# Group 0 taken in one piece before group 1's row work: an order change at the head of a routed expert layer

## The reference

```
x  = x + layernorm(x) @ W          # W: 256 x 256, set from the edge list (src, dst, weight)
z  = layernorm(x)
xn = layernorm(z) * gamma + beta
w  = softmax of the 2 largest of (xn @ Wr + br), 0 for the other 6 experts
x  = x + sum over e of w[e] * (gelu(xn @ W1[e] + b1[e]) @ W2[e] + b2[e])
```

## Time and profile before

| | |
|---|---|
| median of 3 runs | 1067.41 us (1066.4 to 1067.57) |
| the profiled execution | 1067.55 us, its span 1065.8 us |
| busy, share of the span | PE 85%, PEld 79%, DVE 71%, ACT 59%, POOL 59% |
| stretch of the 196 sends on POOL | 139.6 to 390.7 us |
| third stage on PE | from 395.9 us to the end |
| mean granted TensorE clock | 0.919 of full speed |

### The profile page before, as it was taken

One profiled execution on the slowest core, in us unless ns is written; L12 is line 12 of the kernel. 1 busy time (PEld: TensorE's weight loads), 2 busy tenths in 40 slices (PEclk: granted clock), 3 DMA queues, 4 the chain that ended last, 5 costly groups with the idle time before them and its releaser, 6 DMA issues. The chain is left out here.

```text
span 1065.8 us, 25585 instructions
## 1 busy us (share of the span) xinstructions
PE 902.6 (85%) x6756; PEld 842.6 (79%) x6757; DVE 753.5 (71%) x2311; ACT 633.5 (59%) x1324; POOL 630.5 (59%) x490
## 2 busy tenths in 40 slices
PE   1494698898986109999999999999999999999991
PEld 1123577777765109999999999999999999999991
DVE  4995798999984606777777777777777777777761
ACT  2244567666654006667667667667677677677661
POOL 3645057777777752465655655655756565656653
PEclk9797798989986559999999999999999999999996
DMA  4144457757654443465554554554654554555542
GB/s 123 56 127 150 135 161 228 225 195 243 210 168 158 148 162 72 73 99 87 82 95 73 93 94 80 82 96 73 93 92 79 83 95 79 92 85 81 93 67 30
DMA packets 95923, 121.47 MB, mean 114 GB/s; under 512 B 15198, under 2 KB 73734, under 8 KB 95752
## 3 DMA queue, kind: packets, MB, share of 16 engines
q0 software_dynamic: 39904, 53.56, 29.1%
q1 hardware_dynamic: 55976, 67.43, 21.9%
HBM read 51.94 MB, written 69.00 MB: 113 GB/s over the span
## 5 line engine op out<-in xcount | busy, mean ns | idle before, releaser
L574 POOL DMA_INDIRECT out_dram<-ysb,yid x210 | 382.6, 1822 | 283.6 <-ACT ysb L1342 132.9
L744 PE MATMUL psum<-xh,w1s 128*128 128x256 f32 x1680 | 310.9, 285 | 0.0
L744 PEld LDWEIGHTS psum<-xh,w1s 128*128 128x128 f32 x1680 | 257.1, 189 | 0.0
L558 POOL DMA_INDIRECT slots<-arena_z,pos x196 | 191.8, 978 | 89.8 <-issue 58.8
L757 PE MATMUL psum<-w2h,hl 128*128 x840 | 237.5, 283 | 0.0
L757 PE MATMUL psum<-w2l,hh 128*128 x840 | 237.3, 283 | 0.0
L757 PE MATMUL psum<-w2h,hh 128*128 x840 | 237.2, 282 | 0.0
L744 PE MATMUL psum<-xl,w1s 128*128 128x256 f32 x840 | 235.3, 280 | 0.0
L1159 DVE TENSOR_TENSOR hl<-hact,hh 128x512 fp32r<-128x512 f32 x210 | 145.6, 693 | 88.0 <-ACT hh L1206 87.8
L1206 ACT ACTIVATE xh<-psum 128x512 fp32r<-128x512 f32 x105 | 62.7, 597 | 221.3 <-PE psum L731 221.3
L1325 ACT ACTIVATE hact<-psum,b1T 128x256 f32<-128x256 f32 x420 | 174.5, 466 | 14.2 <-PE psum L744 2.8
(11 more groups left out here) (186 smaller groups left out, 1123.8 us busy)
## 6 DMA issues: line engine op xcount, KB each, us to landing
zin<-slots SPq DMA_DIRECT2D x105, 260.0 KB
arena_x<-in_x_dram SPq DMA_DIRECT2D x14, 512.0 KB, 5.4
out_dram<-arena_s SPq DMA_DIRECT2D x14, 512.0 KB
arena_z<-in_L_ffn_W_dram SPq DMA_DIRECT2D x24, 256.0 KB, 2.8
arena_x<-in_x_dram SPq DMA_DIRECT2D x13, 384.0 KB
out_dram<-arena_s SPq DMA_DIRECT2D x13, 384.0 KB
out_dram<-ysb,yid POOLq DMA_INDIRECT x210, 4.3
slots<-arena_z,pos POOLq DMA_INDIRECT x196
```

Source lines behind the costliest of these rows:

```text
L558: pool.indirect_dma_start(slots[:, :], bass.IndirectOffsetOnAxis(ap=pos[b][0:n, k, s:s + 1], axis=0), zg[b][0:n, s, :], None).then_inc(sen ...
L574: pool.indirect_dma_start(out[:, :], bass.IndirectOffsetOnAxis(ap=yid[u % MB][:, n:n + 1], axis=0), ysb[u % YB][:, n, :], None, compute_op ...
L744: last = nc.tensor.matmul(bank[2 + 2 * b + q][:, m * PAIR:(m + 1) * PAIR], w1s[b][:, w, k, hb * P:(hb + 1) * P], xs[b][:, k * PAIR:(k + 1) ...
```

## The change

On each of three engines the order of groups 0, 1 and 2 is rewritten; nothing is computed otherwise. PE does group 0's whole z side right behind its x side, then the first half of group 1's x side with `ranks(0)` in it, then the rest. DVE does group 0 with nothing filled in, then `x_scales` of group 1, the route and the place of group 0, each as one run, and then group 1 with `x_scales` of group 2 filled in and no route. Group 2 holds the route of group 1 and no place; group 3 holds the place of group 1, as it did. ACT follows PE. SP's and POOL's programs are not touched.

```diff
@@ PE
-            group(1, 1, older=False)
-            for g in range(2, GROUPS):
+            for q in range(NP):
+                turn_z(0, q, 0)
+                if q > 0:
+                    logits(0, q - 1)
+            logits(0, NP - 1)
+            turn_x(1, 0)
+            turn_x(1, 1)
+            edge_product(1, 0)
+            ranks(0)
+            turn_x(1, 2)
+            turn_x(1, 3)
+            for q in range(1, NP):
+                edge_product(1, q)
+            group(2, 0, older=False)
+            for g in range(3, GROUPS):
@@ DVE
-                scales = iter(()) if last else x_scales(g + 1, 1 - b, loads)
-                router = iter(()) if first else route(g - 1, (g - 1) % RZ)
-                places = iter(()) if g < 2 else place(g - 2, (g - 2) % RZ)
+                scales = iter(()) if first or last else x_scales(g + 1, 1 - b, loads)
+                router = iter(()) if g < 2 else route(g - 1, (g - 1) % RZ)
+                places = iter(()) if g < 3 else place(g - 2, (g - 2) % RZ)
...
             group(0, 0, first=True)
+            for steps in (x_scales(1, 1), route(0, 0), place(0, 0)):
+                for _ in steps:
+                    pass
             group(1, 1)
@@ ACT
-            group(1, 1, older=False)
-            for g in range(2, GROUPS):
+            act.wait_ge(z_scale_ready, 1)
+            for s in range(4):
+                z_norm(0, s, 0)
+            z_copy(0, 0)
+            z_norm(0, 4, 0)
+            z_norm(0, 5, 0)
+            z_copy(0, 1)
+            z_norm(0, 6, 0)
+            z_copy(0, 2)
+            z_copy(0, 3)
+            act.wait_ge(x_scale_ready, 2)
+            for s in range(3):
+                x_norm(1, s, 1)
+            x_copy(1, 0)
+            x_norm(1, 3, 1)
+            x_norm(1, 4, 1)
+            x_copy(1, 1)
+            exp_gap(0)
+            x_norm(1, 5, 1)
+            x_norm(1, 6, 1)
+            x_copy(1, 2)
+            x_copy(1, 3)
+            group(2, 0, older=False)
+            for g in range(3, GROUPS):
```

## The result

The changed kernel takes 1077.8 us (median, 1076.97 to 1078.44) against 1067.49 us before (1065.48 to 1068.36) in the same comparison: a ratio of 1.0098 [1.0085, 1.0111], slower by 1%. The forecast was 1076.5 us, between 1070.5 and 1080. The profiled execution of the changed kernel took 1077.85 us with a span of 1076.1.

The account below looks back on a forecast made before the run. POOL's unbroken sends were taken to bound the group stage. Stretches up to group 1's first send summed to 166.6 against 157.5, +9.1 us: 1067.55 + 9.1 = 1076.65, set at 1076.5 us against the median, range 1070.5 to 1080.

Parts of the forecast that it names:

- The bound and the one-for-one end: POOL's unbroken sends limit the group stage; the kernel's end moves one for one with the last send.
- Steps 1 to 5: Group 0's statistics, z side, route, ranks and place run alone: released at 129.0 instead of 138.67, 9.7 us earlier.
- step 1: Group 0's statistics and root on DVE end at 110.0, bounds 109.3 and 110.8; stall beside POOL 0.7 us at most.
- Step 6: On DVE, group 1's adds stand behind group 0's place: x_scale_ready at 137.8, 8.8 us after group 0's release.
- Steps 7 and 8: Group 1 released at 165.7, sent at 166.6; POOL idle from 147.8, never starving again; end moves +9.1 us.
- step 7: From group 1's x_scale_ready to its release, with group 2's work between: 27.9 us, bounds 24.5 and 29.
- Rival B: PE reaches 2.4 GHz sooner: half or more, 1065.4 to 1069.5, chance 0.08; less than half, 1069.6 to 1073, 0.15.
- The lower bounds: Fast ends at 2.4 GHz: z side 5.6 us, product and ranks 4.5, x_scale_ready to group 1's release 24.5.
- step 2: Group 0's z side alone on PE and ACT: 10.2 us at 1.2 GHz, 5.6 us at 2.4 GHz.
- B's full case: All of PE's work in the lower bounds at 2.4 GHz: -2.1 us, 1065.4; chance 0.08 together with about half of it.

Follow-up runs that it names:

- hold_first_sends: The changed kernel with POOL's sends of group 0 held until group 1's z scale is ready: 1077.44 us, ratio 1.0083 to the kernel before.
- route_place_spread: The changed kernel with DVE filling in group 0's route and place as before, PE and ACT unchanged: 1076.58 us, ratio 1.007 to the kernel before.
- the last kernel: The changed kernel with extra products on PE behind group 0, ahead of group 2 and in the gaps: 1069.78 us, ratio 1.0007 to the kernel before.

## Why the prediction was right

**The bound and the one-for-one end.** It said that the end moves with group 1's first send and not with group 0's. hold_first_sends shows it: group 0's first send moved by 11 us, and the time stayed. route_place_spread moved it by 20, to where POOL just ran without a break again, and the time did not rise either. Group 1's send moved by 10.36 us and the profiled time by 10.3.

**Steps 1 to 5.** S at 110.96, against 110.0; the first stage's own shift is 1.2 us, so without it S would lie 0.2 us ahead of the forecast. Five steps of the root took 1.12 to 1.20 us instead of 0.17 beside POOL's subtractions, the stall that step 1 allowed for. The z side alone took 121.15 - 110.96 = 10.19 us (forecast 10.2). `chosen_ready` came at 125.0 (L1001 ran from 124.7, 0.29 long), forecast 124.1 from a route at 120.3, the same 3.8 us. The ranks were waited for 2.56 us, forecast 3, and the place took 1.65 (forecast 1.8). Group 0 was released at 129.54, forecast 129.0. Taking the price of a stretch from the one place in the old trace where the same work ran alone and at the same clock, group 13's, was what made these come out.

**Step 6.** From group 0's release to `x_scale_ready`: 138.17 - 129.54 = 8.63 us, forecast 8.8. The size was right, its cause only in part. I said that the place, with its wait for the ranks, holds group 1's adds. route_place_spread shows the adds waiting for PE as long, less about 1.4 us: PE's second product would not have been there sooner. The hold is on PE and ACT, which begin group 1's x side at 120.96 and 119.07 instead of 111.97 and 110.83.

**Steps 7 and 8.** 138.17 to 167.04 is 28.87 us, forecast 27.9, bounds 24.5 and 29: near the slow bound, with the clock at 0.57 in the middle of it. DVE waited there for ACT's z norms (4.24 us) and not for the loads that moved. POOL was idle for 19.77 us, forecast 166.6 - 147.8 = 18.8, and no second hole followed. Group 1's send at 167.86 against 166.6: S lay 1.0 us later, step 7 took 1.0 more, the steps between 0.7 less.

**Rival B, tested by force.** The lower bounds (5.6, 4.5 and 24.5 us) would have put group 1's send at 155.4. With PE at 2.4 GHz from 100 to 165 us it came at 158.58 from an S of 109.92. Two of the three bounds held: from the logits' end to the ranks 122.59 - 118.05 = 4.5 us, and from `x_scale_ready` (132.87) to the release (157.76) 24.9. The second of these held by a looser working than the first: it halved the whole 6.5 us, the waits for ACT with them. The z side's did not hold: 118.05 - 109.92 = 8.1 us and not 5.6. Halving PE's busy time leaves ACT's chain of norms and copies, whose last copy ends at 116.33, 6.4 us after S, with the last logits still to come. A part of the 8.1 us is the extra products themselves, which stand in the z side's gaps; how much was not measured. So the term that was mis-sized is the lower bound of step 2: in this form B's full case was worth 1069.8 us and not 1065.4.

**How much is order and how much is clock.** With PE kept busy in both kernels the ratios differ by 1.0007 - 0.9976 = 0.0031 to 1.0007 - 0.9964 = 0.0043, 3.3 to 4.6 us; the second counterpart also holds the early place. In the profiles, from S to group 1's first send, they differ by 48.66 - 46.83 = 1.8 us and 48.66 - 43.95 = 4.7 us. As they are, the kernels differ by 0.0098, 10.4 us. By these differences the order itself costs some 2 to 5 us, and the rest, some 6 to 8, comes from the clock that the new order's straight chain is run at (0.50 in 111 to 126, 0.57 in 139 to 147). The figures come from different comparisons, and the counterparts did not have the full clock throughout either (0.89 in 111 to 126 with 25 products): the share is measured only that roughly, and the order's may be larger. Which gap of PE gives back how much was not separated, nor whether it was the filled gaps or the kind of the added work that kept the clock.

The Trainium skill ("TensorE: Matmul & The Clock Gate", section "Part 1: The HAM clock gate") says that the throttled state is the default and that activity releases it. These runs agree: the same z side was granted 0.50 as it stands and 1.00 with extra products ahead of it and in its gaps. They show besides that being busy was not enough: as it stands, PE was busy for 12.72 of 15 us and was not released.

## What to carry to other kernels

Where a queue runs without a break from its second batch on, the date of its second batch counts, and a first batch that is sent earlier only makes a hole. Before driving one group straight through, ask what stands behind it on each in-order engine, and price it by the trace of a place where that chain runs alone, at the clock granted there. Taking two interleaved groups apart can be paid twice: in the waits that each had hidden for the other, and in the clock that TensorE is then granted.

## What had not been expected

- The clock fell in the middle of a z side in which PE hardly idled: 13.10 busy us of 15, 0.66 granted, eight products of the same shapes 1.05 and then 1.72 us. With extra products in the gaps as well it stayed at 1.00, and the kernel was 9.7 us faster by the ratios than the changed kernel as it stands, while doing more work.
- The kernel before gains 0.24% [0.09, 0.39] from 25 products that nothing reads, and 0.36% [0.24, 0.48] with nine more and one place moved. The trace shows the second gain (group 1's send 2.7 us earlier after S) and not the first.
- DVE's last shift ahead of S took 1.19 us in the last kernel instead of 0.17, beside POOL's subtraction of 1.27 us that began 0.10 us before it. It is the stall that step 1 allowed for, on another instruction; the Trainium skill ("SBUF — State Buffer", section "SBUF: two separate sides") names VectorE instructions with two SBUF inputs among those that block against GpSimd reading SBUF, and this row agrees.
